# A transformer's layer-norm roots: from VectorE to GpSimd, and one residual ahead of a strip's sums

## The chip, the cores and the metric

The kernel runs on one core of one Trainium2 chip. The metric is the device time of one execution in microseconds, the median of several runs. The engines of the core are TensorE (PE), VectorE (DVE), ScalarE (ACT), GpSimd (POOL) and the DMA queues, issued mostly from SyncE (SP).

## The reference

Four layers in a row on x of 4 x 64 x 128 x 128 float32. The first, third and fourth are box convolutions and aren't touched. The second, `L1_conv`, is four AFNO blocks, and the change lies in it:

```python
def _ln(x, w, b, eps=1e-05):
    mu = jnp.mean(x, axis=-1, keepdims=True)
    v = jnp.mean((x - mu) ** 2, axis=-1, keepdims=True)
    return (x - mu) * jax.lax.rsqrt(v + eps) * w + b

def _block(x, ...):                      # x: (4, 64, 128, 128), four such blocks
    xn = _ln(jnp.transpose(x, (0, 2, 3, 1)), ln1w, ln1b)
    xf = jnp.fft.rfft2(xn, axes=(1, 2), norm='ortho')
    # two complex 64 x 64 mixes with bias, relu after the first, small values masked after the second
    xs = jnp.fft.irfft2(xc, s=(H, W), axes=(1, 2), norm='ortho')
    x = residual + jnp.transpose(xs, (0, 3, 1, 2))
    xp2 = _ln(jnp.transpose(x, (0, 2, 3, 1)), ln2w, ln2b)
    h = jax.nn.gelu(xp2 @ mw1 + mb1, approximate=False)
    m = h @ mw2 + mb2
    return x + jnp.transpose(m, (0, 3, 1, 2))
```

## The kernel before

The kernel is written with raw engine queues and semaphores. Each engine has its own program, and within an engine the order is that of the code. The function `afno_layers` handles 4 images x 4 blocks = 16 runs (`RUNS`). The loop `periods()` goes over runs n = -2 to 16 and, in each, over 16 steps q (`BLOCKS`), each with four slots s. In step q of period n three things are woven together: the MLP of block Q = 16 n + q of run n (8 rows of 128 x 64), the spectrum of run n + 1 (forward DFT in steps 4 and 5, mixing and masking in steps 5 to 10, backward DFT around step 11, inverse DFT from step 12 into steps 0, 1 and 4 of the next period), and the sums of squares for both layer norms. `parts(n, q, s, ...)` picks the spectrum's pieces by slot. The steps in `CLOSED` (0, 1, 7, 8, 9, 11) put the MLP's pieces at other slots than the rest.

The layer norm needs an inverse deviation for each pixel. `sum_up` on VectorE sums a strip of 16 rows (part 0, line 1452) and its squares (part 1, line 1455; ScalarE's `square`, line 1593, writes them into the single buffer `sq` and so waits for `s_sq_read`, the count of sums done). The array `stat` has four planes (sum, sum of squares, variance, inverse root) and `SETS` = 4 sets. One "root" handles one set: 2 x 32 values a partition where both norms have data, 32 at the two ends of the run. There are 70 of them (r = -7 to 62). Before the change `root` runs on VectorE: twelve small instructions of `root_step` (lines 986 to 1006), each waiting for the one before; an integer guess, one cubic step, one Newton step. The root of number 4 n + 3 stands in step 14 behind the residual, 4 n in step 1, 4 n + 1 in two halves in steps 5 and 6, 4 n + 2 in two halves in step 9. After the last operation VectorE counts up `s_root` (line 1469).

What follows a root:

- GpSimd's `normalise(Q + 2)` (line 1275) in slot 0 of every step. Every fourth block waits for `s_root`. It writes y2, TensorE's `turn` (line 1759) transposes it one step later, ScalarE's `operand` (line 1565) copies it, and TensorE's `mlp_up` (line 1739), ScalarE's `gelu` (line 1559), `mlp_down` (line 1750), ScalarE's `mlp_delta` (line 1572), TensorE's `turn_back` (line 1765) and VectorE's `residual` (line 1433) follow. `mlp_down` waits for the residual of the block before, since both use the PSUM bank `result`; `mlp_up` of a half waits for the gelu of the half before, since `wide` is single.
- GpSimd's `next_y` (line 1287), the first norm's operand for the run after, and `fold` (lines 1297 to 1300).

GpSimd's queue also holds `inverse` (lines 1262 and 1263: the upper rows of the inverse DFT, released by VectorE's even rows of lines 1371 and 1372 and ScalarE's copy `odd`) and `masked` (lines 1313 and 1317, behind VectorE's mask of lines 1419 and 1422), for which the backward DFT (line 1729) waits.

## Time and profile before

| what | value |
|---|---|
| median of 3 runs | 3560.59 us (3559.42 to 3563.01) |
| profiled execution | 3561.85 us, span 3560.0 us |
| mean granted TensorE clock | 0.963 of full |
| TensorE busy | 3248.4 us (91%) |
| VectorE busy | 2393.6 us (67%) |
| ScalarE busy | 2205.7 us (62%) |
| GpSimd busy | 1649.7 us (46%) |

The span is the time from the first instruction to the last on the core. Busy is the time in which an engine worked; waits and semaphore instructions don't count. The AFNO layer lies between about 205 and 3140 us of the span, the box convolutions around it.

### The profile page before, as it was taken

The page shows a single profiled execution, that of the slowest core. Times are in us where ns is not written, and L with a number is a line of the kernel's source. Part 1 is how long each engine was busy: PE and PEld are TensorE (multiplying, and loading weights), DVE is VectorE, ACT ScalarE, POOL GpSimd, SP SyncE. Part 2 cuts the span into 40 slices and gives each one's busy share as a digit, 9 for nine tenths or more (in the row PEclk, how much of TensorE's full clock was granted, in tenths as well). Part 3 has the DMA queues.
Part 4 walks back from the last instruction along what each step waited for, and adds up shares of the span by engine and source line. Part 5 has one row for each costly group of instructions (what it writes and reads, how often), then busy time and mean ns, then how long its engine had stood idle before and what let it go on. Part 6 is the DMA issues. An engine that isn't in the chain of part 4 may idle for free. (4 is left out here: it accounts for less than half of the span.)

```text
span 3560.0 us, 52776 instructions
## 1 busy us (share of the span) xinstructions
PE 3248.4 (91%) x18285; PEld 1965.7 (55%) x18285; DVE 2393.6 (67%) x4148; ACT 2205.7 (62%) x3477; POOL 1649.7 (46%) x1389
## 2 busy tenths in 40 slices
PE   6946699999999999998999999999999999979689
PEld 2735464647474646464647464646474747334257
DVE  4956666767676676766667667676767665536677
ACT  3954466666666666666666666666656565646468
POOL 4435545464646454545454645455454543210242
PEclk7967899999999999999999999999999999999889
DMA  9850001010101011313120101111111111356898
GB/s 324 275 187 24 30 31 62 34 65 31 66 31 66 31 66 37 118 48 137 48 89 31 66 31 65 37 60 44 57 42 54 42 54 42 147 188 190 262 303 239
DMA packets 250279, 334.08 MB, mean 94 GB/s; under 512 B 22304, under 2 KB 195616, under 8 KB 242608
## 3 DMA queue, kind: packets, MB, share of 16 engines
q1 hardware_dynamic: 241664, 315.29, 26.3%
q0 software_dynamic: 7904, 15.57, 1.6%
q8 instruction: 144, 2.36, 0.3%
q14 instruction: 103, 0.84, 0.1%
q10 hardware_dynamic: 464, 0.02, 0.0%
HBM read 188.06 MB, written 142.74 MB: 93 GB/s over the span
## 5 line engine op out<-in xcount | busy, mean ns | idle before, releaser
L1559 ACT ACTIVATE images<-a_wide,a_up_b 128x1024 f32<-128x1024 f32 x512 | 569.8, 1113 | 247.2 <-PE a_wide L1739 245.8
L1739 PE MATMUL a_wide<-images 64*128 64x512 f32 x2048 | 579.2, 641 | 23.8 <-ACT images L1559 23.1
L1317 POOL TENSOR_TENSOR images<-a_o,a_mag 128x256 f32<-128x256 f32 (+1 forms) x512 | 360.6, 731 | 378.3 <-DVE a_mag L1422 378.3
L1750 PE MATMUL a_result<-images 128*64 128x512 f32 x2048 | 499.0, 607 | 34.8 <-DVE images L1433 34.8
L1275 POOL TENSOR_TENSOR images<-images,a_stat 128x512 f32<-128x512 f32 x256 | 268.6, 1050 | 545.7 <-DVEq L1469 527.0
L1402 DVE TENSOR_TENSOR a_o<-a_bank,a_mix_b 128x512 f32<-128x512 f32 (+1 forms) x272 | 180.9, 665 | 249.6 <-PE a_bank L1714 246.7
L1705 PEld LDWEIGHTS a_bank<-a_dft_h,a_g 128*128 128x128 f32 x2080 | 273.5, 192 | 129.9 <-issue 129.9
L1433 DVE TENSOR_TENSOR images<-a_result,images 128x512 f32<-128x512 f32 x256 | 175.6, 686 | 224.8 <-PE a_result L1765 224.6
L1750 PEld LDWEIGHTS a_result<-images 128*64 128x64 f32 x2048 | 128.6, 136 | 355.6 <-issue 339.9
L1739 PEld LDWEIGHTS a_wide<-images 64*128 64x128 f32 x2048 | 156.7, 185 | 287.8 <-issue 258.0
L1455 DVE TENSOR_REDUCE a_stat<-a_sq 128x16 f32<-128x1024 f32 x240 | 290.7, 1211 | 10.5 <-ACT a_sq L1593 8.6
L1696 PE MATMUL a_bank<-a_xf,a_mix_fold 128*128 128x512 f32 (+1 forms) x544 | 286.4, 608 | 5.8 <-ACT a_xf L1546 5.8
L1685 PE MATMUL a_bank<-dft_w,images 128*128 128x128 f32 x2048 | 246.2, 279 | 48.4 <-POOL images L1300 46.2
L1263 POOL TENSOR_TENSOR images<-images,a_odd 128x512 f32<-128x512 f32 (+1 forms) x128 | 161.6, 1263 | 270.1 <-DVE images L1372 260.8
L1572 ACT ACTIVATE images<-a_result,a_down_b 128x512 f32<-128x512 f32 x256 | 175.8, 687 | 176.6 <-PE a_result L1750 176.1
L1452 DVE TENSOR_REDUCE a_stat<-images 128x16 f32<-128x1024 f32 x232 | 281.5, 1213 | 4.8
L1685 PEld LDWEIGHTS a_bank<-dft_w,images 128*128 128x128 f32 x2048 | 235.4, 193 | 84.2 <-POOL images L1300 46.3
L1705 PE MATMUL a_bank<-a_dft_h,a_g 128*128 128x128 f32 x2080 | 278.3, 276 | 1.8 <-DVE a_g L1395 1.8
L1593 ACT ACTIVATE a_sq<-images 128x1024 f32<-128x1024 f32 x216 | 227.3, 1052 | 68.8 <-DVE a_stat L1455 43.0
L1729 PE MATMUL a_bank<-a_dft_hi,images 128*128 128x128 f32 x2048 | 235.4, 277 | 8.9 <-POOL images L1317 8.9
L1729 PEld LDWEIGHTS a_bank<-a_dft_hi,images 128*128 128x128 f32 x2048 | 232.3, 194 | 12.8 <-POOL images L1317 12.8
L1520 ACT ACTIVATE a_g<-a_bank 64x252 f32<-64x252 f32 (+3 forms) x512 | 166.6, 374 | 77.5 <-PE a_bank L1685 58.2
(206 smaller groups left out, 6119.7 us busy)
## 6 DMA issues: line engine op xcount, KB each, us to landing
rows<-images SPq DMA_DIRECT2D x112, 512.0 KB, 2.6
images<-rows SPq DMA_DIRECT2D x105, 512.0 KB, 3.7
box_xc<-in_x SPq DMA_DIRECT2D x16, 1024.0 KB, 16.7
box_x<-in_x SPq DMA_DIRECT2D x64, 256.0 KB, 4.3
turned<-box_o SPq DMA_DIRECT2D x64, 256.0 KB, 3.6
images<-turned SPq DMA_DIRECT2D x16, 1024.0 KB, 11.8
planes<-box_work SPq DMA_DIRECT2D x64, 256.0 KB, 3.7
box_xc<-planes SPq DMA_DIRECT2D x16, 1024.0 KB, 19.2
```

The source lines that it names most:

```text
L1275: G.tensor_tensor(rows(y2[:, i % 2]), x[:, row:row + HB], r[:, :, None].broadcast_to([P, HB, C]), ALU.mult).then_inc(s_y2, 1)
L1317: ins = G.tensor_tensor(y[n % 2][:, :, to].rearrange("p c k -> p k c"), o2[:, j % 3, lo:4, r], mask[:, lo:4], ALU.mult)
L1452: V.tensor_reduce(to, strip, AX.X, ALU.add)
L1455: V.tensor_reduce(to, squares_of(r, kind, u), AX.X, ALU.add).then_inc(s_sq_read, 1)
L1559: A(hidden[:, i % 2, j], wide[:], ACT.Gelu, bias=up_b2[:, l, j:j + 1]).then_inc(s_hid, 1)
L1593: A(squares_of(r, kind, u), strip, ACT.Square).then_inc(s_sq, 1)
L1685: mm = M(bank[i % 4][:, c * P:(c + 1) * P], y[n % 2][:, 4 * i + c, :], dft_w[:], start=True, stop=True)
L1696: M(bank[2][:, 0:cols], mix1_fold[:, l], xf[:, 0:cols], start=True, stop=True).then_inc(s_mix1, 1)
L1705: mm = M(bank[0][:, k * P:(k + 1) * P], g[:, first_kw(t) + k].rearrange("p r c -> p (r c)"), dft_h[:], start=True, stop=True)
L1729: mm = M(bank[i % 4][:, c * P:(c + 1) * P], y[n % 2][:, 4 * i + c, :], dft_hi[:], start=True, stop=True)
L1739: mm = M(wide[:, half * BANK:(half + 1) * BANK], up_fold[cs, l, j * P:(j + 1) * P], yc[cs, i % 2], start=True, stop=True)
L1750: mm = M(result[half * C:(half + 1) * C, :], down[:, l, j, :], hidden[:, i % 2, j, half * BANK:(half + 1) * BANK], start=j == 0, stop=j == ...
```

## The change

`root` moves from VectorE's program to GpSimd's. Its twelve operations become nine: the variance times C squared (a product, a scaled sum of squares, a difference, a clamp with epsilon), a power with exponent -0.5 out of a new tile `half`, and one Newton step of four operations. GpSimd runs the root of number 4 n in step 2, 4 n + 1 in step 6 and 4 n + 3 in step 14, each in slot 0 right before `normalise(Q + 2)`, and 4 n + 2 in step 9 in two parts, four operations in slot 2 and five in slot 3. `sum_up` on VectorE now waits for the root of the set's last use before it writes the set again. On VectorE the sums of the strip of step 13 (second norm's lower, first norm's upper: kind 2, u = 1) move into step 14, behind the residual of that step.

```diff
--- before.py
+++ after.py
@@ -851,9 +851,7 @@
 SETS = 4
 RUNS = B * L
 N_WLOAD = 26
-RSQRT_GUESS = 0x5F3759DF
-CUBIC = 3.0 / 8.0
-ROOT_STEPS = 12
+ROOT_STEPS = 9
 
 
 
@@ -975,35 +973,31 @@
     return n if kind is None else n + [(k, v) for k, v, _ in strips_of(r)].index((kind, u))
 
 
-def root_step(nc, dve, step, n, view, j):
-
-
-    V = nc.vector
+def root_step(nc, pool, step, n, half, view, j):
+
+
+    G = nc.gpsimd
     total, total_sq, v, r = (view(q) for q in range(4))
     if j:
-        dve.wait_ge(step, n[0])
+        pool.wait_ge(step, n[0])
     if j == 0:
-        ins = V.scalar_tensor_tensor(out=v, in0=total, scalar=-1.0 / (C * C), in1=total, op0=ALU.mult, op1=ALU.mult)
+        ins = G.tensor_tensor(v, total, total, ALU.mult)
     elif j == 1:
-        ins = V.scalar_tensor_tensor(out=v, in0=total_sq, scalar=1.0 / C, in1=v, op0=ALU.mult, op1=ALU.add)
+        ins = G.tensor_scalar(total_sq, total_sq, float(C), None, ALU.mult)
     elif j == 2:
-        ins = V.tensor_scalar(v, v, 0.0, LN_EPS, ALU.max, ALU.add)
+        ins = G.tensor_tensor(v, total_sq, v, ALU.subtract)
     elif j == 3:
-        ins = V.tensor_scalar(r.bitcast(I32), v.bitcast(I32), 1, None, ALU.logical_shift_right)
+        ins = G.tensor_scalar(v, v, 0.0, C * C * LN_EPS, ALU.max, ALU.add)
     elif j == 4:
-        ins = V.tensor_scalar(r.bitcast(I32), r.bitcast(I32), -1.0, float(RSQRT_GUESS), ALU.mult, ALU.add)
-    elif j in (5, 9):
-        ins = V.tensor_tensor(total, r, r, ALU.mult)
+        ins = G.tensor_tensor(r, v, half[:, :, None].broadcast_to(v.shape), ALU.pow)
+    elif j == 5:
+        ins = G.tensor_tensor(total, r, r, ALU.mult)
     elif j == 6:
-        ins = V.tensor_tensor(total, total, v, ALU.mult)
+        ins = G.tensor_tensor(total, total, v, ALU.mult)
     elif j == 7:
-        ins = V.scalar_tensor_tensor(out=total, in0=total, scalar=-10.0 / 3.0, in1=total, op0=ALU.add, op1=ALU.mult)
-    elif j == 8:
-        ins = V.scalar_tensor_tensor(out=r, in0=total, scalar=5.0, in1=r, op0=ALU.add, op1=ALU.mult)
-    elif j == 10:
-        ins = V.scalar_tensor_tensor(out=total, in0=total, scalar=-0.5 * CUBIC ** 3, in1=v, op0=ALU.mult, op1=ALU.mult)
+        ins = G.tensor_scalar(total, total, -0.5 * C, 1.5 * C, ALU.mult, ALU.add)
     else:
-        ins = V.scalar_tensor_tensor(out=r, in0=total, scalar=1.5 * CUBIC, in1=r, op0=ALU.add, op1=ALU.mult)
+        ins = G.tensor_tensor(r, r, total, ALU.mult)
     n[0] += 1
     return ins.then_inc(step, 1)
 
@@ -1059,6 +1053,7 @@
         mag = sb("mag", [P, 2, 4, 2, C])
         ends = sb("ends", [P, 2, 2, C])
         stat = sb("stat", [P, 4, SETS, 2, 2 * SH])
+        half = sb("half", [P, 1])
         ident = kept["ident"]
         dft_w = kept["dft_w"]
         dft_h, dft_hi, idft_e, idft_o, sym_e, sym_o = (
@@ -1082,7 +1077,7 @@
         s_spill, s_reload = [sem(f"spill{i}") for i in range(8)], [sem(f"reload{i}") for i in range(8)]
         s_stage_out = [sem(f"stage_out{i}") for i in range(2)]
         s_stage = sem("stage")
-        s_step, s_act_step = sem("step"), sem("act_step")
+        s_step, s_act_step, s_root_step = sem("step"), sem("act_step"), sem("root_step")
         s_sq, s_sq_read, s_root, s_y, s_fold = (sem(n) for n in ("sq", "sq_read", "root", "y", "fold"))
         s_zero, s_fw, s_g_dve, s_g_act = (sem(n) for n in ("zero", "fw", "g_dve", "g_act"))
         s_fh, s_xf, s_mix1, s_o1, s_mix2, s_o2 = (sem(n) for n in ("fh", "xf", "mix1", "o1", "mix2", "o2"))
@@ -1228,6 +1223,8 @@
             @block.gpsimd
             def _(pool):
                 G = nc.gpsimd
+                count = [0]
+                chain(pool, s_root_step, count, G.memset(half[:], -0.5))
                 with nc.allow_non_contiguous_dma("small weights"):
                     loads = [(centre, const[CENTRE])]
                     for t, n in ((mix1, "w1"), (mix2, "w2")):
@@ -1265,6 +1262,20 @@
                 def other(n, i):
                     pass
 
+                def root(r, js):
+                    lo, hi = 0 if has_second(r + 1) else 1, 2 if has_first(r + 7) else 1
+                    if js[0] == 0:
+                        pool.wait_ge(s_sq_read, squares_before(r + 1))
+                        if has_second(r - 3):
+                            pool.wait_ge(s_y2, 4 * (r - 3) + 4)
+                        if has_first(r + 3):
+                            pool.wait_ge(s_y, 2 * (r + 3) + 2)
+                    for j in js:
+                        root_step(nc, pool, s_root_step, count, half, lambda p: stat[:, p, r % SETS, lo:hi, :], j)
+                        if j == ROOT_STEPS - 1:
+                            pool.wait_ge(s_root_step, count[0])
+                            pool.sem_inc(s_root, 1)
+
                 def normalise(i):
                     if i % 4 == 0:
                         pool.wait_ge(s_root, i // 4 - 1 - FIRST_ROOT + 1)
@@ -1322,8 +1333,13 @@
                     Q = BLOCKS * n + q
                     m, k = (n, q // 4 - 1) if q >= 4 else (n - 1, SETS - 1)
                     comes = -2 <= m and m + 2 < RUNS
+                    r = SETS * n + (q - 2) // 4
                     for s in range(4):
                         parts(n, q, s, inverse, other, spectrum, other)
+                        if s == 0 and q in (2, 6, 14) and FIRST_ROOT <= r < END_ROOT:
+                            root(r, range(ROOT_STEPS))
+                        if s >= 2 and q == 9 and FIRST_ROOT <= r + 1 < END_ROOT:
+                            root(r + 1, (range(ROOT_STEPS // 2), range(ROOT_STEPS // 2, ROOT_STEPS))[s - 2])
                         if s == 0 and 0 <= Q + 2 < BLOCKS * RUNS:
                             normalise(Q + 2)
                         late = 1 if q == 10 else 0
@@ -1443,6 +1459,8 @@
                         strip = strip_of(n, k, u)
                     to = stat[:, part, r % SETS, kind - 1, u * SH:(u + 1) * SH]
                     if part == 0:
+                        if r - SETS >= FIRST_ROOT:
+                            dve.wait_ge(s_root, r - SETS - FIRST_ROOT + 1)
                         if kind == 1:
                             dve.wait_ge((s_x, s_x_up)[u], INVERSES * n + 2 * k + 2)
                         elif fresh(n):
@@ -1454,22 +1472,8 @@
                         dve.wait_ge(s_sq, squares_before(r, kind, u) + 1)
                         V.tensor_reduce(to, squares_of(r, kind, u), AX.X, ALU.add).then_inc(s_sq_read, 1)
 
-                def root(r, js):
-                    lo, hi = 0 if has_second(r + 1) else 1, 2 if has_first(r + 7) else 1
-                    if js[0] == 0:
-                        dve.wait_ge(s_sq_read, squares_before(r + 1))
-                        if has_second(r - 3):
-                            dve.wait_ge(s_y2, 4 * (r - 3) + 4)
-                        if has_first(r + 3):
-                            dve.wait_ge(s_y, 2 * (r + 3) + 2)
-                    for j in js:
-                        root_step(nc, dve, s_step, count, lambda p: stat[:, p, r % SETS, lo:hi, :], j)
-                        if j == ROOT_STEPS - 1:
-                            dve.wait_ge(s_step, count[0])
-                            dve.sem_inc(s_root, 1)
-
                 for n, q in periods():
-                    Q, r = BLOCKS * n + q, SETS * n + q // 4
+                    Q = BLOCKS * n + q
                     if (n, q) == (-2, 0):
                         scale_weights()
                     if (n, q) == (-2, 10):
@@ -1479,9 +1483,11 @@
                     parts(n, q, 0, inverse, forward, spectrum, backward)
                     if q not in CLOSED and 0 <= Q - 2 < BLOCKS * RUNS:
                         residual(Q - 2)
-                    if q == 14 and FIRST_ROOT <= r < END_ROOT:
-                        root(r, range(ROOT_STEPS))
-                    strips = (strips_at(n, 12)[1:] if q == 13 else []) + strips_at(n, q)[:1]
+                    if q == 14:
+                        for strip in strips_at(n, 13)[:1]:
+                            sum_up(*strip, 0)
+                            sum_up(*strip, 1)
+                    strips = strips_at(n, 12)[1:] if q == 13 else strips_at(n, q)[:1]
                     late = (2 if q in CLOSED else 3) if q == 5 or q % 4 == 3 and fresh(n) else 1
                     for s in range(1, 4):
                         parts(n, q, s, inverse, forward, spectrum, backward)
@@ -1493,13 +1499,6 @@
                         if s == late + 1 and q in CLOSED:
                             for strip in strips:
                                 sum_up(*strip, 1)
-                        if FIRST_ROOT <= r < END_ROOT:
-                            if q == 1 and s == (2 if q in CLOSED else 1):
-                                root(r, range(ROOT_STEPS))
-                            if (q, s) in ((5, 3), (9, 2)):
-                                root(r, range(ROOT_STEPS // 2))
-                            if (q, s) in ((6, 1), (9, 3)):
-                                root(r, range(ROOT_STEPS // 2, ROOT_STEPS))
 
             @block.scalar
             def _(act):
```

## Rows read from the trace of the kernel before

**Rows 1.** Windows: stretch, length, busy time of each engine, granted clock, DMA.
```profile
1057.57:1070.72 13.15, 12.86 (x66) 6.02 (x66) 10.93 (x25) 7.19 (x9) 7.12 (x11) 1.00 0.01 1
1092.80:1267.24 174.44, 169.65 (x973) 102.85 (x972) 122.11 (x216) 110.16 (x164) 91.17 (x77) 1.00 0.14 49
```

**Rows 2.** TensorE's waits, 568 to 3030: total us, times, longest.
```profile
PE a_result L1750 <- DVE images L1433: 32.4, 42, 2.0
PE a_turned L1759 <- POOL images L1275: 17.4, 25, 1.1
```

**Rows 3.** Timeline of VectorE: start, us, instruction, idle before it.
```profile
999.33 1.21 DVE L1455 TENSOR_REDUCE a_stat<-a_sq 128x16 f32<-128x1024 f32 x1
...
1109.01 0.68 DVE L1433 TENSOR_TENSOR images<-a_result,images 128x512 f32<-128x512 f32 x1
...
1112.36 0.23 DVE L1006 SCALAR_TENSOR_TENSOR a_stat<-a_stat 128x64 f32<-128x64 f32 x1
...
1128.41 1.22 DVE L1455 TENSOR_REDUCE a_stat<-a_sq 128x16 f32<-128x1024 f32 x1
...
1133.07 0.69 DVE L1371 TENSOR_TENSOR images<-a_bank,images 128x512 f32<-128x512 f32 x1
```

**Rows 4.** Timeline of TensorE, the backward DFT's start and steps 14 to 4.
```profile
1070.72 14.56 PE L1729 MATMUL a_bank<-a_dft_hi,images 128*128 128x128 f32 x128 [0.29 <-POOL images L1317]
...
1106.45 0.66 PE L1765 MATMUL a_result<-ident,images 128*128 128x128 f32 x4
...
1109.84 1.94 PE L1750 MATMUL a_result<-images 128*64 128x512 f32 x8 [0.88 <-DVE images L1433]
1111.70 1.13 PE L1739 MATMUL a_wide<-images 64*128 64x512 f32 x4
...
1113.82 0.66 PE L1759 MATMUL a_turned<-ident,images 128*128 128x128 f32 x4 [0.40 <-POOL images L1275]
...
1118.97 0.66 PE L1765 MATMUL a_result<-ident,images 128*128 128x128 f32 x4
...
1145.82 0.66 PE L1759 MATMUL a_turned<-ident,images 128*128 128x128 f32 x4 [1.04 <-POOL images L1275]
```

**Rows 5.** Timeline of GpSimd, the start-up and one period.
```profile
259.14 2.81 POOL L1287 TENSOR_TENSOR images<-images,a_stat 128x1024 f32<-128x1024 f32 x1 [1.97 <-DVEq L1469]
261.92 2.82 POOL L1287 TENSOR_TENSOR a_upper<-images,a_stat 128x1024 f32<-128x1024 f32 x1
264.82 2.33 POOL L1298 TENSOR_TENSOR images<-images,a_upper 128x1024 f32<-128x1024 f32 x1
...
1008.21 1.04 POOL L1275 TENSOR_TENSOR images<-images,a_stat 128x512 f32<-128x512 f32 x1 [26.25 <-DVEq L1469]
...
1112.72 1.04 POOL L1275 TENSOR_TENSOR images<-images,a_stat 128x512 f32<-128x512 f32 x1 [7.43 <-DVEq L1469]
...
1134.50 1.27 POOL L1263 TENSOR_TENSOR images<-images,a_odd 128x512 f32<-128x512 f32 x1 [4.43 <-DVE images L1372]
...
1138.07 1.05 POOL L1275 TENSOR_TENSOR images<-images,a_stat 128x512 f32<-128x512 f32 x1
...
1144.71 1.05 POOL L1275 TENSOR_TENSOR images<-images,a_stat 128x512 f32<-128x512 f32 x1
```

**Rows 6.** One tile's operations on GpSimd: count, duration ns min/median/max.
```profile
L1262 POOL TENSOR_TENSOR images<-images,a_odd x16: 319/320/322, 396.1 to 3029.7; 128x64 f32<-128x64 f32 x16
...
L1297 POOL COPY images<-a_upper x16: 294/418/423, 252.3 to 2783.9; 128x64 f32<-128x64 f32 x16
```

**Rows 7.** Timeline of ScalarE, steps 14 and 15.
```profile
1109.19 1.06 ACT L1593 ACTIVATE a_sq<-images 128x1024 f32<-128x1024 f32 x1 [1.00 <-DVE a_stat L1455]
...
1115.71 1.06 ACT L1593 ACTIVATE a_sq<-images 128x1024 f32<-128x1024 f32 x1 [0.60 <-DVE images L1433]
```

**Rows 8.** The root's operations on VectorE: count, ns min/median/max.
```profile
L996 DVE TENSOR_TENSOR a_stat<-a_stat x140: 191/224/227, 244.9 to 3111.9; 128x64 f32<-128x64 f32 x116, 128x32 f32<-128x32 f32 x24
...
L988 DVE SCALAR_TENSOR_TENSOR a_stat<-a_stat x70: 191/224/2356, 244.0 to 3110.1; 128x64 f32<-128x64 f32 x58, 128x32 f32<-128x32 f32 x12
```


## The prediction

> **What bounds the kernel now.** I read the span in steady stretches first. One image-layer takes 174.4 us, and in it TensorE is busy for 169.7 us at full granted clock, VectorE for 122 and GpSimd for 91 [rows 1]. So only 4.8 us of each of these periods can be won at all, and taking 12 operations off VectorE shortens nothing by itself. I then asked what ends TensorE's waits over 14 of the periods: the residual of line 1433 on VectorE comes first (32.4 us, 42 times) and the normalisation of line 1275 on GpSimd second (17.4 us, 25 times) [rows 2]. Both lie in the part of a period that runs from step 14 to step 4, where no DFT fills the gaps. The timelines show how. The reader is to see two knots.
>
> Knot A, step 14. VectorE finishes the last sum of a strip just before 1109.1, adds the residual (1109.01) and runs the root to 1112.6 (last operation 1112.36 + 0.23) [rows 3]. TensorE's down projection waits 0.88 us for that residual, and its next turn waits for the normalisation that the root released (1112.72, 1.04 long), at 1113.82 [rows 4, 5].
>
> Knot B, steps 1 to 4. The root follows the sum of 1128.41 on VectorE and holds back the even rows of line 1371 to 1133.07. These release GpSimd's add at 1134.50, then come a fold, the normalisation of block 4 at 1138.07, 5.7 us of next_y, and the normalisation of block 5 at 1144.71, for which TensorE's turn at 1145.82 waits 1.04 us [rows 3 to 5].
>
> **The price of the root on GpSimd.** Call X the time from the root's first instruction to the release of s_root. Five of its nine operations are two-input forms on 64 elements a partition. The form stands in the trace on GpSimd at this very size: line 1262, 320 ns [rows 6]. So 5 x 0.32 = 1.60 us. Three are one-input forms; the trace has none of a packed row, so I bound them by half and by the whole of the two-input form (0.16 to 0.32) and take 0.25, nearer to the whole, since GpSimd's smallest copy of 64 elements takes 0.29 [rows 6]: 0.75 us. Each operation waits for the one before. GpSimd's own dependent step is in the trace: next_y from 261.92 lasts 2.82, and the fold that waits for it starts at 264.82, 0.08 late, where an independent instruction starts slightly before the end of the last (259.14 + 2.81 against 261.92) [rows 5]. Nine waits with the last before s_root: 0.72 us. The power P isn't in the trace. It can't be under a plain two-input form (0.32), and I put the far end at ten such forms, 3.2. I take 1.0, the geometric middle of the two (three forms' worth); this is the weakest number here. X = 1.60 + 0.75 + 0.72 + 1.0 = 4.1 us, between 3.1 (one-input forms at 0.16, P at 0.32) and 6.3. On VectorE the chain takes 3.0 us.
>
> The Trainium skill, GPSIMD Engine Reference, section Elementwise — side-by-side cycle accounting, says that VectorE needs about 1 cycle an element and GpSimd about 2.6 for two inputs, and measures 1.96 between them. By that ratio nine of twelve operations would take 3.0 x 9/12 x 1.96 = 4.4 us, an estimate from the page; it speaks against the change and gives about my sum. The trace has 320 ns against 224 for the two-input form at 64 elements [rows 6, 8], a milder 1.4, because at this size the fixed part counts.
>
> **Knot A after the change.** Residual first: the instruction can start when its transpose is done (1106.45 + 0.66), so near 1107.15 instead of 1109.01, and the 0.88 gap before the down projection goes. But the strip's sums move behind it and end near 1110.1 instead of 1109.1, and ScalarE's next square waits for that read (it waited 1.00 us for it already, starting at 1109.19) [rows 7]. Behind the square stands gelu(Q,1), and the next up projection waits for it: 1110.1 + 1.1 + 1.1 = 1112.3, against 1111.7 before. So the gain of 0.88 isn't kept by TensorE. GpSimd starts the root at 1110.2, normalises at 1110.2 + X, and the turn follows 1.1 later at 1111.3 + X. With 4.1 that is 1115.4 against 1113.82: later by X - 2.5. After the turn something is given back: from it to the next transpose 5.15 us passed (1113.82 to 1118.97) [rows 4], of which about 0.6 was a square that waited for VectorE's late residual (1115.71, 0.60 idle) [rows 7]; VectorE is ahead now. Knot A: X - 3.1, and never below -0.5, since the square holds TensorE anyway.
>
> **Knot B after the change.** Line 1371 follows the sum at once, at 1129.6, 3.5 us earlier; GpSimd's add starts at 1131.0 and its fold ends at 1134.6. There the root stands in front of both normalisations: 1134.6 + X instead of 1138.07, so both are later by X - 3.5. The turn of block 5 moves by the same. The residual that VectorE delivered late (0.89 of the same kind) is on time, but TensorE then waits at the turn. Knot B: X - 3.5, not below -2.4, where TensorE's own work binds.
>
> **The other two roots.** At step 6 GpSimd idled 26.25 us before the normalisation of 1008.21, though the sums were done at 1000.5 (999.33 + 1.21) [rows 3, 5]; a root of up to 7.5 us is hidden there, and the next_y behind it gains. At step 9 the halves stand between products of line 1317 that the backward DFT waits for. From the end of the last sum, 1057.57, to TensorE's start of that DFT lie 13.15 us in which GpSimd is busy for 7.12 [rows 1], so 6 us are free, and TensorE waits 0.29 at the end [rows 4]. An X of 4.1 is hidden; from about 6 it shows. Without this cover each would cost its X.
>
> **The sum.** A and B together: 2X - 6.6 a period, which breaks even at X = 3.3. With 4.1 it is +1.6 us, over 15 periods +24. In the start-up GpSimd builds the first two images alone: three of four roots ran under its own folds and left gaps near 1.97 (before 259.14) [rows 5]; the 32-element roots now stand in its queue at some 3.2 us (estimate: forms of 0.25 and 0.2, half of P at 64 elements, the same waits), about +4 with the first. The first period's spectrum, where the root's halves on VectorE held TensorE, gives about 3.5 back. The last period and this add +2. The memset of the exponent and the new wait in sum_up (for a root four strips back) cost nothing; no DMA or queue of SP's moves. 3561.85 + 24 + 2 = 3588 for the profiled execution; its span is 3560.0, and it lies 1.3 above the median of the runs, so 3587 for the median. All 70 chains [rows 8] leave VectorE, some 210 us of its busy time, for nothing.
>
> **The rivals.**
> *Faster.* GpSimd's chain is no longer than 2.5 us, shorter than VectorE's (forms of 0.2, waits that overlap). Then A gives -0.5 and B -1.0, and 15 x -1.5 = -22: 3539. For it: no row shows a packed one-input form on GpSimd, and eight of the nine waits rest on one dependent pair of long instructions. Against it: the exact two-input form at 320 ns makes 1.6 us alone. It decides below X = 3.07, where 15 x (2X - 6.6) reaches -7.
> *No change to be measured.* P as cheap as an ordinary form, X = 3.1 to 3.5: 15 x (-0.4 to +0.4) is -6 to +6, so 3555 to 3567.
> *Long power.* P of 3.2 makes X = 6.3, +6 a period, +90, and step 9 begins to show: 3650 or more. The lock adds to this: a root operation on VectorE once took 2356 ns where its median is 224 [rows 8], in the start-up, while GpSimd ran folds. A VectorE instruction can thus be held for the length of a GpSimd one, and the compare of line 1422 in step 9 could be held by the power; VectorE has about 1.1 us free a chunk, so P of 3.2 would cost 2 us a period more, 30 in all: 3680.
> The Trainium skill, SBUF — State Buffer, section SBUF: two separate sides, calls that pair an exclusive lock, held for the whole instruction; by it P = 1.0 costs nothing here, and the trace agrees by the 2356 ns.
>
> **How the numbers follow.** 0.2% (7 us) is about what a measurement can tell from no change. Forecast (X 3.5 to 6, 3568 to 3640): 0.47. Long power: 0.11. No change: 0.22. Faster: 0.20. Low end 3550 keeps half of the faster case; the high end 3635 leaves out the long power. Slower 0.58, same 0.22, faster 0.20. Likeliest 3587.
>
> **What would show it.** In a steady period: VectorE busy 122 less 12; GpSimd busy 91 plus some 13; the gap of line 1750 gone; turn waits of line 1759 on line 1275 grown from 1.4 to near 4 us a period; X read from the first operation of a root to the normalisation behind it. I am wrong if P is far from 1.0, if dependent steps cost other than 0.08, or if line 1371 doesn't move ahead by 3.5.

## The result

The changed kernel takes 4138.22 us (median of 4, 4136.73 to 4142.27) against 3561.8 (3559.42 to 3563.05) for the kernel before on the same chip: 16.2% slower, ratio 1.1624 [1.1609, 1.1638]. The forecast was 3587, and its range ended at 3635. The sign was right and the size was not.

The page of the changed kernel, first and second part (busy us and share of the span, instructions; then TensorE's granted clock in 40 slices, in tenths):

```profile
PE 3355.9 (81%) x18285; PEld 2015.0 (49%) x18285; DVE 2200.2 (53%) x3308; ACT 2208.8 (53%) x3477; POOL 2498.1 (60%) x2020
...
PEclk7958898989898989898989999999999999998979
```

VectorE gave up 193 us (2393.6 before). GpSimd took on 848 (1649.7 before). TensorE, whose matmuls nobody touched, has 107 us more (3248.4 before). The costliest groups on GpSimd say where the 848 went, and TensorE's waits between 627 and 3597 us (total, times, longest) say who paid; they answer to [rows 2]:

```profile
L992 POOL TENSOR_TENSOR a_stat<-a_stat,a_half 128x64 f32<-128x64 f32 (+1 forms) x70 | 677.5, 9679 | 4.5
```

```profile
PE a_turned L1758 <- POOL images L1286: 413.1, 55, 12.6
PE a_wide L1738 <- ACT images L1558: 31.5, 44, 1.6
PE a_bank L1728 <- POOL images L1328: 23.4, 14, 2.1
```

Line 992 is the power: 70 instructions, 677.5 us. The residual (line 1449 now), first in [rows 2] with 32.4 us, is gone from the list. In its place the turn waits for GpSimd's normalisation: 413.1 us where it was 17.4.

One steady period; the stretch of it from just before the end of its first long wait to behind its second; and the matmuls right behind the first wait (stretch; length, then busy us of PE, PEld, DVE, ACT, POOL; granted clock, DMA share and GB/s), against [rows 1]:

```profile
1052.23:1263.87 211.64, 176.84 (x973) 105.91 (x972) 111.22 (x168) 110.32 (x164) 143.46 (x113) 0.92 0.12 40
1084.00:1130.00 46.00, 33.72 (x130) 12.80 (x131) 17.32 (x19) 22.52 (x27) 38.29 (x24) 0.79 0.20 61
1084.76:1090.66 5.90, 5.90 (x17) 1.99 (x17) 1.22 (x1) 2.66 (x3) 5.90 (x3) 0.57 0.31 89
```

The period grew by 37.2 us (174.44 to 211.64). TensorE's idle time in it grew from 4.8 to 34.8, so 30.0; its busy time for the same 973 instructions grew by 7.2, and the granted clock fell from 1.00 to 0.92. The forecast had a term for the first and none for the second.

GpSimd's timeline, step 14 (start, us, instruction, idle before it), against the normalisation of 1112.72 in [rows 5]:

```profile
1069.59 0.29 POOL L984 TENSOR_TENSOR a_stat<-a_stat 128x64 f32<-128x64 f32 x1 [4.88 <-DVE a_stat L1473]
1069.97 0.38 POOL L986 TENSOR_SCALAR a_stat<-a_stat 128x64 f32<-128x64 f32 x1
1070.44 0.32 POOL L988 TENSOR_TENSOR a_stat<-a_stat 128x64 f32<-128x64 f32 x1
1070.85 0.43 POOL L990 TENSOR_SCALAR a_stat<-a_stat 128x64 f32<-128x64 f32 x1
1071.37 10.55 POOL L992 TENSOR_TENSOR a_stat<-a_stat,a_half 128x64 f32<-128x64 f32 x1
1082.00 0.29 POOL L994 TENSOR_TENSOR a_stat<-a_stat 128x64 f32<-128x64 f32 x1
...
1083.11 0.32 POOL L1000 TENSOR_TENSOR a_stat<-a_stat 128x64 f32<-128x64 f32 x1
1083.66 1.04 POOL L1286 TENSOR_TENSOR images<-images,a_stat 128x512 f32<-128x512 f32 x1 [0.24 <-POOLq L1277]
```

X, from the first operation to the normalisation, is 1083.66 - 1069.59 = 14.07 us, where the forecast had 4.1. All but 3.5 of it is one instruction of 10.55 us. TensorE's timeline of the same period, against [rows 4]:

```profile
1071.81 1.13 PE L1738 MATMUL a_wide<-images 64*128 64x512 f32 x4 [1.56 <-ACT images L1558]
...
1084.76 1.11 PE L1758 MATMUL a_turned<-ident,images 128*128 128x128 f32 x4 [11.23 <-POOL images L1286]
...
1122.43 1.11 PE L1758 MATMUL a_turned<-ident,images 128*128 128x128 f32 x4 [11.24 <-POOL images L1286]
...
1237.57 1.12 PE L1758 MATMUL a_turned<-ident,images 128*128 128x128 f32 x4 [5.75 <-POOL images L1286]
```

These are knot A (11.23), knot B (11.24) and step 9 (5.75). Read the duration beside the wait: the turn that took 0.66 us in [rows 4] takes 1.11 after such a wait. The mean of 0.79 over the 46 us from 1084 means about 19 us at the lower level of 1.2 GHz (a share of 0.42, since each us there takes off half of one). Half of them cost nothing, because TensorE was waiting; the other half lay in matmuls, some 5 us behind each wait (0.57 over the 5.90 us from 1084.76), and each us of these costs half a us.

### The profile page after: what moved, and what is told of

The parts are those of the page before. It is cut to its first block and busy times, and to the rows that moved or that the text cites. A ratio compares the mean times of both kernels' runs of the same rounds, so it can differ in the third digit from the quotient of the medians.

```text
span 4136.6 us, 52817 instructions
## 1 busy us (share of the span) xinstructions
PE 3355.9 (81%) x18285; PEld 2015.0 (49%) x18285; DVE 2200.2 (53%) x3308; ACT 2208.8 (53%) x3477; POOL 2498.1 (60%) x2020
## 3 DMA queue, kind: packets, MB, share of 16 engines
q8 instruction: 144, 2.36, 0.2%
## 5 line engine op out<-in xcount | busy, mean ns | idle before, releaser
L992 POOL TENSOR_TENSOR a_stat<-a_stat,a_half 128x64 f32<-128x64 f32 (+1 forms) x70 | 677.5, 9679 | 4.5
L1738 PE MATMUL a_wide<-images 64*128 64x512 f32 x2048 | 608.4, 671 | 39.3 <-ACT images L1558 38.6
L1758 PE MATMUL a_turned<-ident,images 128*128 128x128 f32 x1024 | 178.6, 303 | 461.8 <-POOL images L1286 461.8
L1749 PE MATMUL a_result<-images 128*64 128x512 f32 x2048 | 520.7, 631 | 0.9 <-DVE images L1449 0.9
L1564 ACT ACTIVATE images<-a_turned 128x512 f32<-128x512 f32 x256 | 152.8, 597 | 505.4 <-PE a_turned L1758 505.4
L1758 PEld LDWEIGHTS a_turned<-ident,images 128*128 128x128 f32 x1024 | 130.4, 154 | 479.4 <-POOL images L1286 478.6
L1260 POOL TENSOR_TENSOR images<-images,a_odd 128x512 f32<-128x512 f32 (+1 forms) x128 | 161.2, 1259 | 247.7 <-DVE images L1388 238.5
L1728 PE MATMUL a_bank<-a_dft_hi,images 128*128 128x128 f32 x2048 | 264.7, 298 | 35.4 <-POOL images L1328 35.4
L1728 PEld LDWEIGHTS a_bank<-a_dft_hi,images 128*128 128x128 f32 x2048 | 261.6, 213 | 41.5 <-POOL images L1328 41.5
```

Of the source, the lines that this page charges most:

```text
L992: ins = G.tensor_tensor(r, v, half[:, :, None].broadcast_to(v.shape), ALU.pow)
L1728: mm = M(bank[i % 4][:, c * P:(c + 1) * P], y[n % 2][:, 4 * i + c, :], dft_hi[:], start=True, stop=True)
L1738: mm = M(wide[:, half * BANK:(half + 1) * BANK], up_fold[cs, l, j * P:(j + 1) * P], yc[cs, i % 2], start=True, stop=True)
L1749: mm = M(result[half * C:(half + 1) * C, :], down[:, l, j, :], hidden[:, i % 2, j, half * BANK:(half + 1) * BANK], start=j == 0, stop=j == ...
L1758: mm = nc.tensor.transpose(turned[:, h * P:(h + 1) * P], y2[:, i % 2, h * P:(h + 1) * P], ident[:])
```

## The experiments

**One: everything but the power.** The changed kernel, with an ordinary one-input form where the power stood. It leaves out the power, so its layer norms aren't computed.

```diff
-        ins = G.tensor_tensor(r, v, half[:, :, None].broadcast_to(v.shape), ALU.pow)
+        ins = G.tensor_scalar(r, v, 0.0, 1e-3, ALU.mult, ALU.add)
```

> The changed kernel with the power left out: in its place stands a one-input operation that writes the constant 0.001 (so the norms aren't computed; all instructions, waits and places else stay). Theory 1, the length of the power: the trace after shows a root of 14.05 us from its first operation to the normalisation, of which the power is 10.55. Without it X = 14.05 - 10.55 + 0.43 = 3.9 us, and the prediction's sum 2X - 6.6 gives +1.2 us a period, 15 periods +18, and about +2 at the ends: 3581, at most 3600. Theory 2, the place: GpSimd's queue order, its waits and VectorE's lost order cost the time, and the power only part: above 3700. If the constant of 6.6 is too small (more stalls go than I counted), the time falls below 3560.

Measured: 3572.36 us (3571.75 to 3574.85), ratio to before 1.0035 [1.0021, 1.0049]. Without its power the same change costs 0.35%, 11 us; the power alone costs the other 566. The expectation was 3581, 9 us more. One period of this kernel (windows), TensorE's waits over its periods, its timeline in step 14, and GpSimd's root there, first operation and normalisation:

```profile
1091.44:1266.80 175.36, 169.61 (x973) 102.57 (x972) 109.83 (x168) 109.82 (x164) 102.45 (x112) 1.00 0.14 49
```

```profile
PE a_turned L1758 <- POOL images L1286: 46.5, 39, 2.3
PE a_wide L1738 <- ACT images L1558: 31.5, 44, 1.6
```

```profile
1107.53 1.94 PE L1749 MATMUL a_result<-images 128*64 128x512 f32 x8
...
1111.03 1.13 PE L1738 MATMUL a_wide<-images 64*128 64x512 f32 x4 [1.56 <-ACT images L1558]
...
1113.65 0.66 PE L1758 MATMUL a_turned<-ident,images 128*128 128x128 f32 x4 [0.91 <-POOL images L1286]
```

```profile
1108.81 0.29 POOL L984 TENSOR_TENSOR a_stat<-a_stat 128x64 f32<-128x64 f32 x1 [4.89 <-DVE a_stat L1473]
...
1112.56 1.04 POOL L1286 TENSOR_TENSOR images<-images,a_stat 128x512 f32<-128x512 f32 x1 [0.24 <-POOLq L1277]
```

X is 3.75 here. The forecast's formula, 2X - 6.6 a period, gives +0.9; the period went from 174.44 to 175.36, +0.92. It holds knot by knot too: against the kernel before, TensorE's turns are later by 0.61 us behind knot A (forecast X - 3.1 = 0.65) and by 0.35 behind knot B (forecast X - 3.5 = 0.25), and steps 6 and 9 add nothing. The down projection starts without a wait, where it had 0.88 in [rows 4], and the up projection behind it waits 1.56 for the gelu: the gain is taken back one instruction later, as knot A of the forecast said.

**Two: the price of a power, by itself.** The changed kernel with five operations ahead of GpSimd's loads: powers of 16, 64 and 256 elements a partition on a base of 2, one of 64 on a base of 5000, and a product of 64.

```diff
+                flat = upper[:].rearrange("p c h -> p (c h)")
+                for base, size, op in ((2.0, 16, ALU.pow), (2.0, 64, ALU.pow), (2.0, 256, ALU.pow), (5000.0, 64, ALU.pow),
+                                       (2.0, 64, ALU.mult)):
+                    chain(pool, s_root_step, count, G.memset(flat[:, 0:256], base))
+                    chain(pool, s_root_step, count, G.tensor_tensor(
+                        flat[:, 512:512 + size], flat[:, 0:size], half[:].broadcast_to([P, size]), op))
```

> The changed kernel with five extra operations on GpSimd ahead of its first loads, each on its own: powers of 16, 64 and 256 elements a partition (base 2, exponent -0.5), 64 elements of base 5000, and a product of 64. From the roots of 64 (10.55 us) and 32 elements (5.45): 0.16 us an element plus 0.35, so 2.9, 10.6 and 41.2 us, and the product 0.3. Rival, the cost depends on the value (iterations or branches): base 5000 differs from base 2. Time of the whole: 4138, plus the extra work if it is on the path, up to 65 us.

Measured: 4199.48 us, one run. The five in GpSimd's timeline (the memsets between them left out):

```profile
210.58 2.94 POOL L1232 TENSOR_TENSOR a_upper<-a_upper,a_half 128x16 f32<-128x16 f32 x1
...
213.97 10.53 POOL L1232 TENSOR_TENSOR a_upper<-a_upper,a_half 128x64 f32<-128x64 f32 x1
...
224.95 41.12 POOL L1232 TENSOR_TENSOR a_upper<-a_upper,a_half 128x256 f32<-128x256 f32 x1
...
266.52 10.52 POOL L1232 TENSOR_TENSOR a_upper<-a_upper,a_half 128x64 f32<-128x64 f32 x1
...
277.49 0.29 POOL L1232 TENSOR_TENSOR a_upper<-a_upper,a_half 128x64 f32<-128x64 f32 x1
```

From 64 to 256 elements the power grows by 30.59 us, so by 0.159 an element a partition, with 0.33 to 0.39 fixed. The two bases tried, 2 and 5000, make no difference (10.53 and 10.52). The product of the same size and operands takes 0.29, a 36th. So it is the operation's own work for each element, not the operand `half`, not a first use and not the data.

**Three and four: where a long power costs.** The changed kernel with the power kept only for the roots of steps 2 and 14, and then only for those of steps 6 and 9; the others have the form of experiment one, so their norms aren't computed.

```diff
-    elif j == 4:
+    elif j == 4 and power:
         ins = G.tensor_tensor(r, v, half[:, :, None].broadcast_to(v.shape), ALU.pow)
+    elif j == 4:
+        ins = G.tensor_scalar(r, v, 0.0, 1e-3, ALU.mult, ALU.add)
...
-                        root_step(nc, pool, s_root_step, count, half, lambda p: stat[:, p, r % SETS, lo:hi, :], j)
+                        root_step(nc, pool, s_root_step, count, half, lambda p: stat[:, p, r % SETS, lo:hi, :], j, r % SETS in (0, 3))
```

In the fourth the last argument is `r % SETS in (1, 2)`.

> The changed kernel with the power kept in the roots of steps 2 and 14 and the constant in its place in those of steps 6 and 9 (half of the norms not computed). Theory 1: 2 x 10.1 us a period more than without any power, plus the slower TensorE clock after such stalls (some 3 to 5 us a period by the trace after): 3581 + 15 x 24 = 3941, and about 20 in the start-up, where all go through GpSimd: 3930 to 3990. Theory 2, that the roots of steps 6 and 9 carry most of the loss since they stand among the masks: below 3850.

> The other half: the power kept in the roots of steps 6 and 9, the constant in its place in those of steps 2 and 14 (half of the norms not computed). A period of the changed kernel is 211.6 us, without any power 175.4, with it at steps 2 and 14 alone 198.0. If the sites add up, this one has 175.4 + (211.6 - 198.0) = 189.0 us a period, so 3572 + 16 x 13.6 = 3790, 3770 to 3810. Theory 1 as predicted held these two sites hidden up to an X of 6 to 7.5 us; with 14 they should show 8.0 (step 9) and 6.5 (step 6) of the length: 14.5 a period, about the same. Rival, the sites share their stalls (a late one hides under the other's): above 3850.

Measured: 3930.91 us and 3774.05 us, one run each; both lie inside what was expected, near the low end. A period of each (windows; the third experiment, then the fourth):

```profile
1192.94:1390.91 197.97, 173.07 (x973) 103.82 (x972) 110.03 (x168) 110.14 (x164) 123.08 (x113) 0.95 0.13 43
```

```profile
1162.54:1350.66 188.12, 172.51 (x973) 104.51 (x972) 111.16 (x168) 110.12 (x164) 122.95 (x112) 0.98 0.14 46
```

| kernel | period | TensorE busy | idle | clock |
|---|---|---|---|---|
| before | 174.44 | 169.65 | 4.8 | 1.00 |
| no power | 175.36 | 169.61 | 5.8 | 1.00 |
| power in 2 and 14 | 197.97 | 173.07 | 24.9 | 0.95 |
| power in 6 and 9 | 188.12 | 172.51 | 15.6 | 0.98 |
| changed | 211.64 | 176.84 | 34.8 | 0.92 |

Steps 2 and 14 give +22.6 over the kernel without a power, steps 6 and 9 +12.8; together 35.4, and the whole change has 36.3. So the sites add up nearly, and none hides another. For 2 and 14 the formula gives twice the power's extra 10.3 us, 20.6; 19.1 came as idle time (24.9 less 5.8) and 3.5 as slower matmuls. Step 6 and step 9 had been counted as hidden up to 7.5 and 6 us; beyond that cover the formula's own bounds give 14.07 - 7.5 = 6.6 and 14.07 - 6 = 8.1, 14.7 together, against 9.8 of idle and 2.9 of slower matmuls, 12.8 in all. TensorE's timeline of the fourth kernel shows where (step 6's turn, then step 9's and the backward DFT):

```profile
1260.85 0.66 PE L1760 MATMUL a_turned<-ident,images 128*128 128x128 f32 x4 [1.53 <-POOL images L1288]
...
1324.21 1.11 PE L1760 MATMUL a_turned<-ident,images 128*128 128x128 f32 x4 [5.75 <-POOL images L1288]
1326.96 16.19 PE L1730 MATMUL a_bank<-a_dft_hi,images 128*128 128x128 f32 x128 [1.63 <-POOL images L1330]
```

Step 9 shows 7.4 of the 8.1 (0.3 of it, at the DFT, stood there before). Step 6 shows 1.5 of the 6.6: its cover was nearer to 12.5 us (14.07 less 1.53) than to the 7.5 read from when the sums were done to when the normalisation began, since the normalisation itself was early for its turn. And the DFT behind the wait of step 9 runs at the slower clock, 16.19 us for the 14.56 of [rows 4].

**Five: the residual alone.** The kernel before, roots on VectorE, with only step 14's residual moved ahead of the strip's sums.

```diff
+                    if q == 14:
+                        for strip in strips_at(n, 13)[:1]:
+                            sum_up(*strip, 0)
+                            sum_up(*strip, 1)
                     if q == 14 and FIRST_ROOT <= r < END_ROOT:
                         root(r, range(ROOT_STEPS))
-                    strips = (strips_at(n, 12)[1:] if q == 13 else []) + strips_at(n, q)[:1]
+                    strips = strips_at(n, 12)[1:] if q == 13 else strips_at(n, q)[:1]
```

> The kernel before with the roots left on VectorE, and only step 14's residual moved ahead of the strip's sums (the root still behind both). Theory 1: the down projection's wait of 0.88 us goes, but the sums end 0.4 later (VectorE waits for the residual's transpose), the root and the turn with them, and ScalarE's square is later too: +0.4 us a period or nothing, 3560 to 3568. Rival, the residual's wait was real loss: -0.9 us a period, 15 periods -13, 3548.

Measured: 3567.22 us (3564.58 to 3571.0), ratio 1.0018 [1.0009, 1.0027]. TensorE's timeline in step 14:

```profile
1109.23 1.94 PE L1754 MATMUL a_result<-images 128*64 128x512 f32 x8
...
1112.73 1.13 PE L1743 MATMUL a_wide<-images 64*128 64x512 f32 x4 [1.56 <-ACT images L1563]
```

The same picture as in experiment one, 0.88 given and 1.56 taken (up projection), with the root still on VectorE. The second part of the change, alone, costs about 6 us (3 to 10 by the interval), inside the 3560 to 3568 expected, and so about half of the 11 us that experiment one shows for the whole change without its power.

**Six: the even rows ahead of the root.** The kernel before, with step 1's root pushed from behind the strip's sum to the step's last slot, behind the even rows of line 1371. It was to give what knot B promises, line 1371 early, without paying GpSimd for the root.

```diff
-                            if q == 1 and s == (2 if q in CLOSED else 1):
+                            if q == 1 and s == 3:
```

> The kernel before with one edit: the root of step 1 runs behind the inverse's even rows (slot 3 in place of slot 2), so GpSimd's add and fold run beside it. Theory 1, knot B is VectorE's order and not VectorE's load: GpSimd's add starts 3.5 us earlier, the normalisation of block 4 at the root's end, some 3.2 us earlier, the turn's wait of 1.04 goes and that of the residual (0.89) shrinks to about 0.5: -1.3 us a period, 16 periods -20, 3541. Rival, the stalls just move to the next wait (ScalarE's gelu or the residual, which now stands behind the root): within 7 us of 3561.

Measured: 3603.49 us (3602.1 to 3603.93), ratio 1.0119 [1.0103, 1.0134]. The expectation, a gain, was missed by 62 us, and the rival, which named the residual behind the root but put it within 7 us of 3561, by more than 35. Timelines of VectorE, GpSimd and TensorE around the root:

```profile
1139.47 0.86 DVE L986 SCALAR_TENSOR_TENSOR a_stat<-a_stat 128x64 f32<-128x64 f32 x1
1140.37 2.33 DVE L988 SCALAR_TENSOR_TENSOR a_stat<-a_stat 128x64 f32<-128x64 f32 x1
...
1145.34 0.69 DVE L1433 TENSOR_TENSOR images<-a_result,images 128x512 f32<-128x512 f32 x1
```

```profile
1138.98 1.27 POOL L1263 TENSOR_TENSOR images<-images,a_odd 128x512 f32<-128x512 f32 x1 [0.78 <-DVE images L1372]
1140.20 2.41 POOL L1300 TENSOR_TENSOR images<-images,a_upper 128x1024 f32<-128x1024 f32 x1
...
1145.33 1.04 POOL L1275 TENSOR_TENSOR images<-images,a_stat 128x512 f32<-128x512 f32 x1 [2.72 <-DVEq L1469]
```

```profile
1146.18 3.20 PE L1750 MATMUL a_result<-images 128*64 128x512 f32 x8 [3.23 <-DVE images L1433]
```

Two things happened. Operations that take 0.22 us at the median [rows 8] took 0.86 and 2.33, each ending 0.1 us after the GpSimd instruction that ran beside it (1.27 and 2.41 long). And the residual of the block then stood behind a root of 5.9 us (1139.47 to 1145.34), so the down projection waited 3.23 for it. The waits are only half of the loss. Over the periods TensorE's waits grew by 20.6 us (81.1 to 101.7 in total), and its busy time in the whole run by 21.1 (3248.4 to 3269.5): the eight matmuls of 1146.18 took 3.20 us where they take 1.94 at full clock, and the granted clock over them was 0.58. Letting one piece of work go first moves the other back, and here the one moved back was needed sooner.

**Seven: fewer operations where they were.** The kernel before, the root on VectorE, with the cubic step's constant folded into its operations and the Newton step dropped: nine operations in place of twelve. The relative error of the inverse deviation is at most 1e-4 by the expectation.

```diff
-ROOT_STEPS = 12
+ROOT_STEPS = 9
...
-    elif j in (5, 9):
+    elif j == 5:
         ins = V.tensor_tensor(total, r, r, ALU.mult)
     elif j == 6:
-        ins = V.tensor_tensor(total, total, v, ALU.mult)
+        ins = V.scalar_tensor_tensor(out=total, in0=total, scalar=CUBIC ** 0.5, in1=v, op0=ALU.mult, op1=ALU.mult)
     elif j == 7:
-        ins = V.scalar_tensor_tensor(out=total, in0=total, scalar=-10.0 / 3.0, in1=total, op0=ALU.add, op1=ALU.mult)
+        ins = V.scalar_tensor_tensor(out=total, in0=total, scalar=-10.0 / 3.0 * CUBIC ** 0.5, in1=total, op0=ALU.add, op1=ALU.mult)
-    elif j == 8:
-        ins = V.scalar_tensor_tensor(out=r, in0=total, scalar=5.0, in1=r, op0=ALU.add, op1=ALU.mult)
...
     else:
-        ins = V.scalar_tensor_tensor(out=r, in0=total, scalar=1.5 * CUBIC, in1=r, op0=ALU.add, op1=ALU.mult)
+        ins = V.scalar_tensor_tensor(out=r, in0=total, scalar=5.0 * CUBIC, in1=r, op0=ALU.add, op1=ALU.mult)
```

> Nine operations in place of twelve, but on VectorE: the kernel before without the Newton step (the cubic step with its factor 3/8 folded in has a relative error of at most 1e-4). The root takes 9 x 0.25 = 2.25 us in place of 3.0. Theory 1, the two knots follow the length of the root wherever it runs: knot A loses the turn's wait of 0.40 and those of 0.29 and 0.16 behind it, knot B moves by 0.75: -1.6 us a period, 15 periods -24, about 3537 (3530 to 3548). Rival, TensorE's gaps are filled by the next wait in line (ScalarE's gelu): within 7 us of 3561.

Measured: 3533.95 us (3533.14 to 3534.32), ratio 0.9925 [0.9911, 0.9938]. It beats both kernels. A period, and TensorE's waits over the periods:

```profile
1080.25:1253.16 172.91, 169.41 (x973) 102.80 (x972) 122.09 (x204) 109.97 (x164) 91.23 (x77) 1.00 0.15 50
```

```profile
PE a_result L1746 <- DVE images L1429: 17.7, 25, 1.3
PE a_wide L1735 <- ACT images L1555: 17.4, 58, 0.8
PE a_turned L1755 <- POOL images L1271: 13.1, 12, 1.1
```

The period is 1.5 us shorter. A root shorter by three operations of 0.26 (0.22 and its wait) is 0.78 less at each knot, so 1.56 for the two. The waits for the residual fell from 32.4 to 17.7 us, those for the normalisation from 17.4 to 13.1 [rows 2]. VectorE's busy time did not fall (122.09 against 122.11) though it has 12 instructions fewer: in the groups by line the mask's compare grew from a mean of 523 ns to 675 in the same period, x17, 2.6 us in all. One of the 17 makes up for it: the first, of 64 elements, took 0.20 us before and 2.90 here (1169.29 to 1172.19), beside GpSimd's next_y of 1169.29 to 1172.14. It shows again that busy time on VectorE isn't what counts here.

## Why the prediction was wrong

**The step that failed: "The power P isn't in the trace. It can't be under a plain two-input form (0.32), and I put the far end at ten such forms, 3.2. I take 1.0".** P is 10.55 us, 33 simple forms. The far end was no bound: no row of the trace has a power, and ten times was a number picked, not read. With P measured and the rest of the working kept, X would be 1.60 + 0.75 + 0.72 + 10.55 = 13.6, and 2X - 6.6 = +20.6 a period; with step 6 at 6.1 and step 9 at 7.6 beyond their cover, +34.3, over 15 periods +515: about 4077 us with start-up and end as forecast. The structure of the sum was sound and would have stood 61 us short of the measured time; its one unknown was off tenfold. That the rest comes so close is in part luck: it has no term for the slower clock (7.2 us a period), and it overcounts step 6 by some 5.

**The rest of X.** Predicted 3.07, measured 3.52 (14.07 less 10.55). The two-input forms were right (0.29 to 0.32 against 0.32), the waits too (0.08 to 0.09: 1069.59 + 0.29 against 1069.97). The three one-input forms were 0.38, 0.43 and 0.25, 1.06 in place of 0.75, and the release of `s_root` 0.24, which the sum had at one wait of 0.08. So the scaling (0.38) and the clamp (0.43) cost more on GpSimd than a product of two tiles, and only the multiply-and-add (0.25) costs less.

**Knots A and B.** The formula 2X - 6.6 was right where it was put to the proof: +0.9 forecast and +0.92 measured at X = 3.75; 19.1 of idle time for 20.6 at X = 14. That the knots follow the root's length on VectorE too is shown by experiment seven: -1.5 for a root that is 0.78 shorter at each. That A doesn't keep the 0.88 us of the residual is shown twice (experiments one and five: 1.56 at the next up projection). In the kernel without the power the two knots are worth +14 over 15 periods, and the whole is +11.

**Steps 6 and 9.** "An X of 4.1 is hidden; from about 6 it shows" held for step 9: TensorE waits 5.75 us at its turn and 1.64 at the backward DFT, and without the power only the 0.3 at the DFT that was there before. Step 6's cover was undersized by some 5 us. Together the two cost 12.8 a period, a third of the loss.

**Start-up and end.** Forecast +2 in all. From the first row of the inverse (line 1259, 1262 before) back to the start the changed kernel has 419.5 against the 396.1 of [rows 6], +23.4: the first four roots there have 32 elements, and their powers of some 5.45 us each stand in GpSimd's queue ahead of the folds. From the last such row to the end it has +9.1 (539.4 against 530.3). Between the first and the last (419.5 to 3597.2 against 396.1 to 3029.7) lie +544.

```profile
L1259 POOL TENSOR_TENSOR images<-images,a_odd x16: 318/324/326, 419.5 to 3597.2; 128x64 f32<-128x64 f32 x16
```

This is the same operation as in [rows 6], by tile (count, ns min/median/max, first and last start): its 324 ns against 320 say that GpSimd itself was no slower.

**What was missing: the clock.** 7.2 of the 37.2 us a period are TensorE's own instructions at a lower clock, and the forecast had no term for them. In the periods shown it fell only in the long waits and behind them: over a period the granted clock was 1.00 with waits up to 1.6 us, 0.98 with one of 5.75, 0.95 with two of 11.2, 0.92 with all three, and TensorE's busy time went up with each (169.6, 172.5, 173.1, 176.8). Much shorter waits can do it: 3.23 us did in experiment six. And the trace of the kernel before had the price, in rows that the forecast didn't read. TensorE's timeline there, in the start-up and in a later period:

```profile
414.54 1.11 PE L1759 MATMUL a_turned<-ident,images 128*128 128x128 f32 x4 [13.48 <-POOL images L1275]
...
1666.87 3.61 PE L1750 MATMUL a_result<-images 128*64 128x512 f32 x8 [1.97 <-DVE images L1433]
```

The first is the turn at 1.11 us behind a wait of 13.48, the second the down projection at 3.61 us (1.94 in [rows 4]) behind one of 1.97; the granted clock over these 3.61 us was 0.53. Two other waits of 1.8 us in that trace had matmuls at full clock behind them, and so had one of 3.20 in experiment six, so the length of the wait by itself doesn't decide; what does stays open here.

**The rivals.** The rival of a long power named the right mechanism and gave it 0.11, at 3650 to 3680; its place and sign were right and its price was a third of the true one. The lock inside it did not come: VectorE's compare in step 9 ran through the power unheld. VectorE's timeline, with GpSimd's power of 1222.88 to 1233.43 beside it:

```profile
1226.61 0.29 DVE L1438 TENSOR_SCALAR a_mag<-a_mag 128x256 f32<-128x256 f32 x1
```

The same compare earlier in the period, on VectorE, and the fold that ran beside it on GpSimd:

```profile
1189.70 2.36 DVE L1438 TENSOR_SCALAR a_mag<-a_mag 128x256 f32<-128x256 f32 x1
```

```profile
1189.59 2.33 POOL L1311 TENSOR_TENSOR images<-images,a_upper 128x960 f32<-128x960 f32 x1
```

So a fold of 2.33 us held this compare, and the power of 10.55 did not. That is no single case: 60 compares of this line ran inside a power in this trace, and none took more than 0.32 us.

By the Trainium skill, SBUF — State Buffer, section SBUF: two separate sides, two kinds of VectorE instruction and a GpSimd instruction shut each other out for the whole of the one that started first: those in a 2-port performance mode, and those with two inputs in SBUF against a GpSimd instruction that reads SBUF. The root operation held for 2.33 us in experiment six, beside a fold of 2.41, agrees with it. The power doesn't fit if the compare is of the first kind, which no run here shows; what is shown is that a fold and next_y held it and powers didn't. How a form with two inputs in SBUF fares beside a power is open: none ran beside one in the changed kernel.

The 4.4 us that the prediction worked out from the ratio in the Trainium skill, GPSIMD Engine Reference, section Elementwise — side-by-side cycle accounting, was near my own sum and just as wrong. That ratio is measured for an add; for the eight ordinary operations it would give 3.9 (8 x 0.25 x 1.96, an estimate from the page) against 3.5 measured, and for the power it says nothing.

**What would show it.** VectorE lost 10.9 us a period (12 forecast), GpSimd gained 11.3 without the power (13 forecast) and 52.3 with it. The residual's gap went and the turn's waits grew, as forecast: from 17.4 us over the periods to 46.5 without the power and 413.1 with it.

## What to carry to other kernels

When a sum has one price that no row shows, and TensorE waits for the work that has this price, the unknown price decides the forecast: write down the length at which each cover is used up (here a root of 3.3, 6 and 7.5 us, where the last proved to be 12.5), and don't give the unknown an upper end made of multiples of a different operation. Count a power on GpSimd by its elements and not as one instruction: a chain of twelve cheap instructions on VectorE was nearly five times quicker (3.0 us against 14.1) than nine with one power among them. And where a change makes TensorE wait longer, look for the slower clock behind the wait: here it added a quarter to the idle time (7.2 on 30), and in experiment six, with waits of 3.2 us, it cost as much as the waits themselves.

## What the runs showed of the hardware

- A power on GpSimd takes 0.159 us for each element of a partition and 0.33 to 0.39 fixed (2.94, 10.53 and 41.12 us for 16, 64 and 256), the same for a base of 2 and of 5000, against 0.29 for a product of 64.
- GpSimd's one-input forms on 64 elements take 0.25 us (multiply and add), 0.38 (multiply) and 0.44 (clamp and add), its two-input ones 0.29 to 0.33.
- Two waits of 11 us and one of 6 in a period of 212 us brought the mean granted clock from 1.00 to 0.92, and to 0.79 in the 46 us from the end of the first of them; the same transposes took 1.11 us there and 0.66 at full clock. Of the waits of 3.2 us in experiment six all but one, and of the waits before the change two of 1.97, had slower matmuls behind them as well (3.20 and 3.61 us for 1.94).
- VectorE's operations of 0.22 us took 0.86 and 2.33 us beside GpSimd instructions of 1.27 and 2.41. A compare of 0.29 took 2.36 beside a fold of 2.33, and never more than 0.32 inside a power of 10.55.
